# A fused decoder layer on one core: passages into and out of the attention stage, and the cross-attention scores on the two halves of the array

## The reference

```python
def reference(x, ctx_1024, ...):
    # self-attention; every row of 1024 scores gets its own maximum (softmax)
    qkv = layernorm(x) @ W_qkv + b_qkv
    energy = einsum('bqhe,bkhe->bqhk', q, k)
    attn = softmax(energy, axis=-1) / sqrt(E)
    x = x + einsum('bihv,bvhd->bihd', attn, v).reshape(B, N, E) @ W_out + b_out
    # cross-attention on 64 context tokens
    q = layernorm(x) @ Wq.T + bq ; k, v = ctx @ Wk.T + bk, ctx @ Wv.T + bv
    scores = einsum('bhqd,bhkd->bhqk', q, k) / sqrt(D_K)
    x = x + (softmax(scores, -1) @ v) @ Wo.T + bo
    # feed-forward, weights rounded to -1, 0, 1 by their mean absolute value
    h = layernorm(gelu(layernorm(x) @ absmean(W_fc).T), ln_w, ln_b)
    return x + h @ absmean(W_proj).T
```

## Time and profile before

| | us |
|---|---|
| three runs | 1186.39, 1189.93, 1192.23 (median 1189.93) |
| the profiled execution | 1189.87 |
| its span, first to last instruction | 1187.9 |
| projections, until the first unit of the attention stage | to about 129 |
| attention | about 129 to 818 |
| last stage | about 818 to 1188 |
| mean granted clock of PE | 0.991 of 2.4 GHz |

### The profile page before, as it was taken

One profiled execution on the slowest core, in us unless ns is written; L12 is line 12 of the kernel. 1 busy time (PEld: TensorE's weight loads), 2 busy tenths in 40 slices (PEclk: granted clock), 3 DMA queues, 4 the chain that ended last, 5 costly groups with the idle time before them and its releaser, 6 DMA issues.

```text
span 1187.9 us, 19073 instructions
## 1 busy us (share of the span) xinstructions
PE 1150.5 (97%) x6532; PEld 593.4 (50%) x6532; DVE 1044.4 (88%) x1974; ACT 861.9 (73%) x1898; POOL 295.6 (25%) x403
## 2 busy tenths in 40 slices
PE   8999999999999999999999999989899999999997
PEld 6544333333333333333333333344467778778777
DVE  5688799999999999999999999975799899899776
ACT  4312588888888888888888888847778778777853
POOL 2124010110110111011011000023565455455431
PEclk9999899999999999999999999989999999999999
DMA  5877113561330331333144000042111121100001
GB/s 175 261 216 233 70 26 45 132 124 21 64 59 7 64 60 29 42 60 51 20 64 66 8 10 7 11 119 61 54 37 38 54 72 34 38 19 18 2 18 36
DMA packets 45920, 74.99 MB, mean 63 GB/s; under 512 B 10112, under 2 KB 23808, under 8 KB 45824
## 3 DMA queue, kind: packets, MB, share of 16 engines
q0 software_dynamic: 9648, 27.27, 13.3%
q1 hardware_dynamic: 36176, 46.50, 12.9%
HBM read 47.53 MB, written 25.69 MB: 62 GB/s over the span
## 4 chain that ended last, share of the span: by engine, by line
PE 84%; DVE 5%; ACT 4%; issue 2%; DMA 2%; POOL 1%; SPq 1%; DVEq 0%; POOLq 0%; ACTq 0%
PE ps L1410 21%; PE ps L1423 21%; PE ps L1257 16%; PE ps L1296 10%; PE ps L1599 4%; PE ps L1519 4%; PE ps L1584 2%; PE ps L1528 2%; ACT ot L715 2%; ACT prob L652 1%; PE ps L1538 1%; DVE xhat L1150 1%; DVE maxes L883 1%; PE ps L1455 1%; ACT pe_ L727 1%
## 5 line engine op out<-in xcount | busy, mean ns | idle before, releaser
L890 DVE TENSOR_REDUCE maxes<-ps 128x1 f32<-128x512 f32 x968 | 607.9, 685 | 34.9 <-PE ps L1296 18.1
L652 ACT ACTIVATE prob<-ps 128x512 f32<-128x512 f32 x1024 | 531.9, 603 | 127.4 <-PE ps L1410 125.8
L1410 PE MATMUL ps<-Qs,Ks 50*128 50x512 f32 x1024 | 377.0, 453 | 5.5 <-DVE parts L915 1.6
L1410 PEld LDWEIGHTS ps<-Qs,Ks 50*128 50x128 f32 x1024 | 168.4, 186 | 315.3 <-ACT prob L652 300.5
L1296 PE MATMUL ps<-Ks,Qs 48*128 48x512 f32 x1024 | 319.3, 431 | 2.7 <-DVE maxes L883 2.6
L1423 PE MATMUL ps<-prob,V_all 128*32 128x512 f32 x2048 | 274.6, 608 | 0.0
L1296 PEld LDWEIGHTS ps<-Ks,Qs 48*128 48x128 f32 x1024 | 166.7, 186 | 46.2 <-DVE maxes L883 15.9
L352 POOL DMA_DIRECT2D Qs<-qk_scratch x90 | 44.4, 500 | 469.1 <-PE ps L1423 468.9
L727 ACT ACTIVATE pe_<-ps,nmx 128x64 f32<-128x64 f32 x512 | 109.7, 367 | 6.3 <-DVE nmx L1069 6.3
L566 POOL TENSOR_TENSOR pe_<-pe_,rsum 128x512 f32<-128x512 f32 x64 | 66.7, 1052 | 61.2 <-DVE rsum L1086 61.2
L1599 PE MATMUL ps<-t_p,fT 128*128 128x256 f32 x512 | 76.7, 293 | 0.0
(11 more groups left out here) (120 smaller groups left out, 1247.1 us busy)
## 6 DMA issues: line engine op xcount, KB each, us to landing
qk_scratch<-parts SPq DMA_DIRECT2D x32, 512.0 KB, 5.1
Qs<-qk_scratch POOLq DMA_DIRECT2D x90, 128.0 KB, 5.2
Ks<-qk_scratch POOLq DMA_DIRECT2D x90, 128.0 KB, 7.5
o_scratch<-ot SPq DMA_DIRECT2D x128, 32.0 KB
on_raw<-o_scratch SPq DMA_DIRECT2D x8, 512.0 KB
r_raw<-r_scratch SPq DMA_DIRECT2D x16, 256.0 KB
x_in<-in_x SPq DMA_DIRECT2D x8, 512.0 KB, 4.0
out<-xo SPq DMA_DIRECT2D x8, 512.0 KB, 2.8
```

The source lines that it names most:

```text
L652: act.activation(prob[:, U % 2, j // 2, j % 2, :], ps[:, ST_BANK[n], :], ACT.Exp).then_inc(exp_done, 1)
L890: dve.tensor_reduce(maxes[:, qc, j * BLK + blk, half:half + 1], ps[:, MAX_BANK["tile", t], :], AX.X, ALU.max).then_inc(max_reduced, 1)
L1410: pe.matmul(ps[:, ST_BANK[n], :], stack(Ks[g], j, ROWS, slice(kb * P, (kb + 1) * P)), stack(Qs[g], j, ROWS, slice(qc * CH, (qc + 1) * CH)) ...
```

## The change: what it does

1. `WARM_UP` goes from 28 to 22.
2. Entry into the attention stage: PE waits for all but the last of the projections' parts before `scores(0, 3)`; the waits for the early maxima and for the last part move into the first unit, behind `scores(1, 1)` and `scores(1, 2)`.
3. The reciprocals of the batches 0 to 2 are taken one by one inside the maxima (after tiles 952, 976 and 1000), and SP writes them ahead of the last `m_rows`.
4. `x_scores` makes two tiles at a time: the keys of heads 0 to 3 of a block lie on partitions 0 to 63 and those of heads 4 to 7 on 64 to 127, and each matmul goes over 64 partitions and 256 columns. `kbd` is half as wide. A tile now holds two row blocks x 4 heads.
5. `x1_apply` (but for chunk 0) and `x2_apply` move from DVE to ACT; POOL makes the negated mean times the factor (`nmr`) for them, two more instructions each.
6. New orders in the last stage on all engines, and a new `RING_PHASE`. On POOL, `normalise` goes from before the last of `probabilities` to between the second and third `rstd_f`; `x2_plus_b` and `x1_plus_b` go to the phase's start. `t2` and `t3` are cut in two.

```diff
-WARM_UP = 28
+WARM_UP = 22
-RING_PHASE = (("s", 2, 0), ("q2", 1, 0), ("s", 3, 0), ("s", 4, 0), ("s", 5, 0), ("s", 6, 0), ("out", 0, 1), ("out", 1, 1),
+RING_PHASE = (("q2", 1, 0), ("s", 2, 0), ("s", 3, 0), ("s", 4, 0), ("s", 5, 0), ("out", 0, 1), ("out", 1, 1), ("pt", 0, 0),
...
+RECIP_TILES = [TILES - 24 * (B - 1 - b) for b in range(B - 1)]
...
# SP, last batch
+                    if last and g == NG - 1:
+                        sp.wait_ge(recip_done, B - 1)
+                        for i in range(B - 1):
+                            r_write(i)
                     m_rows(2 * G + 1, g, 1)
                     if last and g == NG - 1:
-                        sp.wait_ge(recip_done, 1)
-                        for i in range(B - 1):
-                            r_write(i)
                         sp.wait_ge(r_written, 16 * (B - 1))
                         load_o(0, 0)
...
# POOL, rstd_2 (rstd_3 in the same way)
                 pool.tensor_tensor(veps[:, 0], mv[:, 0, :, 1], eps[:], ALU.add).then_inc(veps2_done, 1)
+                pool.tensor_tensor(nmr[:, 0], mv[:, 0, :, 0], minus[:], ALU.mult).then_inc(veps2_done, 1)
...
+                pool.tensor_tensor(nmr[:, 0], nmr[:, 0], rstd[:, 0], ALU.mult).then_inc(nmr2_ready, 1)
...
# ACT (x2_apply in the same way)
+            def x1_apply(c):
+                if not 0 < c < NCH:
+                    return
+                act.wait_ge(nmr2_ready, c + 1)
+                act.wait_ge(t2_done, 2 * c)
+                for blk in range(BLK):
+                    i = act.activation(xn_1[:, blk, :], x1[:, blk, :], ACT.Identity, scale=rstd[:, 0, blk:blk + 1],
+                                       bias=nmr[:, 0, blk:blk + 1])
+                i.then_inc(xn2_ready, 1)
...
# DVE
+            def reciprocals(b):
+                dve.wait_ge(s_loaded, 16 * max(b + 1, B - 1))
+                dve.reciprocal(s_c[:, b, :], s_c[:, b, :]).then_inc(recip_done, 1)
+
             for t in range(EARLY_TILES, TILES):
                 reduce_tile(t)
+                if t in RECIP_TILES:
+                    reciprocals(RECIP_TILES.index(t))
...
-            reciprocals(0, 0, B - 1)
...
+            dve.tensor_tensor(head_mask[:, 0:4], head_mask[:, 0:4], head_mask[:, 4:8], ALU.add).then_inc(prep_done, 1)
...
-                for h in range(8):
+                for h in range(4):
...
# PE
-            pe.wait_ge(parts_ready, 4 * NCH)
-            pe.wait_ge(max_reduced, EARLY_TILES)
+            pe.wait_ge(parts_ready, 4 * NCH - 1)
             scores(0, 3)
...
                 scores(U + 1, 1)
+                if U == 0:
+                    pe.wait_ge(max_reduced, EARLY_TILES)
                 max_tile(t + 2)
                 scores(U + 1, 2)
+                if U == 0:
+                    pe.wait_ge(parts_ready, 4 * NCH)
...
-            def x_scores(c, i):
+            def x_scores(c, t):
                 if not 0 <= c < NCH:
                     return
-                m, blk = divmod(i, BLK)
+                m, pair = divmod(t, 2)
                 pe.wait_ge(q2_copied, 2 * c + m + 1)
-                r = x_bank("s", c, i)
-                pe.matmul(ps[:, r, :], q2T[:, m, blk * P:(blk + 1) * P], kbd[:, c // QC, m * 8 * CTX:(m + 1) * 8 * CTX],
-                          start=True, stop=True).then_inc(s_done, 1)
+                r = [x_bank("s", c, 2 * t + h) for h in range(2)]
+                for k in range(2):
+                    blk = 2 * pair + k
+                    for h in range(2):
+                        rows = slice(h * STRIP, (h + 1) * STRIP)
+                        i = pe.matmul(ps[:, r[h], k * 4 * CTX:(k + 1) * 4 * CTX], q2T[rows, m, blk * P:(blk + 1) * P],
+                                      kbd[rows, c // QC, m * 4 * CTX:(m + 1) * 4 * CTX], start=True, stop=True)
+                        if k == 1:
+                            i.then_inc(s_done, 1)
```

More of the change, by code:

```diff
@@ L747, in o2_copy, with x2_apply @@
                 act.activation(o2T[:, m, :], ps[:, BANK["val", c, m], :], ACT.Copy).then_inc(o2_copied, 1)
+            def x1_apply(c):
[7 more added lines that the diff above has]
+                i.then_inc(xn2_ready, 1)
+            def x2_apply(c):
+                if not 0 <= c < NCH:
+                    return
+                act.wait_ge(nmr3_ready, c + 1)
+                if c:
+                    act.wait_ge(t3_done, 2 * c)
+                for blk in range(BLK):
+                    i = act.activation(xn_2[:, blk, :], x2[:, blk, :], ACT.Identity, scale=rstd[:, 1, blk:blk + 1],
+                                       bias=nmr[:, 1, blk:blk + 1])
+                i.then_inc(xn3_ready, 1)
             def x3_high(c, k):
@@ L1467, in t2 @@
                 pe.wait_ge(xn2_ready, c + 1)
-                for k in range(KT):
-                    transposes(x_bank("t2", c, k), k, xn_1).then_inc(t2_done, 1)
+                transposes(x_bank("t2", c, k), k, xn_1).then_inc(t2_done, 1)
             pe.wait_ge(v_copied, 2 * NCH)
@@ L1551, in t3 @@
                 pe.wait_ge(xn3_ready, c + 1)
-                for k in range(KT):
-                    transposes(x_bank("t3", c, k), k, xn_2).then_inc(t3_done, 1)
+                transposes(x_bank("t3", c, k), k, xn_2).then_inc(t3_done, 1)
             def fc(c, blk):
```

243 lines of the change are left out of this document (125 added, 118 removed), and 6 rows, old and new, of the table RING_PHASE.

## The result

The changed kernel takes 1180.87 us (median of 5 runs, 1179.83 to 1184.37) against 1189.76 for the kernel before in the same comparison: ratio 0.993, 95% interval 0.9913 to 0.9946. It is faster by 9 us, where 24.7 were forecast. The profiled execution has a span of 1180.8 us (before 1187.9).

A forecast was written before the change was run, and what follows sets the result against it. The prediction took DVE to bound attention and PE phases 2 to 6 of the last stage; its terms summed to -24.7 us from the profiled 1189.87, so 1165 us, range 1156 to 1174, or 1156 to 1182 with rivals.

The forecast's parts named there:

- the exit: From attention to the last stage: PE's wait for POOL and the slow clock behind it go, -6.2 us (bounds -3 and -8).
- phase 1: Last stage, second phase: PE's work falls to 30.6 us, 32 to 32.5 with remaining waits, -4.0 us (bounds -1, -5).
- phases 2 to 6: Last stage: PE stays the bound, but blocked f_apply leaves a phase at 42.0 us, -1.75 each, -8.7 for five.
- the end: End of the kernel: x2_apply waits for two more POOL instructions, +0.3 us.
- phase 0: Last stage, first phase: scores 2.4 us less, x1_apply ahead of the last exponentials, -2.5 us (bounds 0, -4).
- the reciprocals: In attention on DVE: taken as three of 128x128 inside the maxima and paid in full, +2.5 us (bounds +1.5, +2.7).
- the entry: Into attention: less DVE idle time before and behind its first maxima, -3.0 us (bounds -0.8 and -3.9).
- The second rival: Way out of attention: gain hidden by a later read or x1_apply(0) under POOL, -2 not -6.2 us, 1172; chance 0.10.
- Scores: Last stage on PE: the array's halves overlap, so scores take 4.0 to 4.2 us, saving 2.7 us a phase.
- the first rival: Last stage's score matmuls: halves don't overlap for two passes, scores cost 0.5 us more a phase, 1183 us; chance 0.10.
- The warm-up: Kernel start: fewer warm-up matmuls let the first transposes start earlier, carried through the projections, -1.1 us (bounds 0, -1.3).
- The rival on the slower side: Last stage: POOL blocks both f_apply of a pair, PE waits 3 us each phase, clock falls, 1199 us; chance 0.04.

## Why the prediction was wrong

The direction was right and 1180.87 lies in the range of 1156 to 1182, but the gain is little over a third of the forecast's. Of the 17.4 us that are missing in the table, 7.3 are the exit, 3.9 phase 1, 3.0 phases 2 to 6, 2.0 the end, 1.5 phase 0, 1.2 the start and 1.0 phase 7; the reciprocals gave 2.1 back and the entry 0.3.

*The exit* is the step that failed: "Late next is ACT, whose exponentials limit the last units, and DVE's `x1_apply(0)`, which ends 6 us sooner as well because `kbd` has 8 instructions and not 16." The first half came true, a projection 6.5 us earlier and without a wait. But x1_apply(0) ended only 4.9 us sooner (810.97 and 806.04), 2.9 of which had been gained before the last maximum, because an earlier `normalise` meets DVE's preparation and costs it 4.1 us, and the apply stayed at 5.45 us under POOL's second pair. So the wait of 3.57 us was in effect not removed but moved on by 13 us, and the low clock went with it. Holding POOL back shows it: 7.1 us. The second rival named this ("`x1_apply(0)` under POOL is last") and had a chance of 0.10; it was also too mild, 4.2 us lost where 7.3 were. The number that spoke for it stood in the earlier trace rows, an apply beside POOL at 4.14 us; the prediction named it for this rival and left it out of the exit's sum. The trace before had the better one, the 5.51 us of x1_apply(0) itself.

*Phase 1* failed next: "In phase 1 DVE is the chain". It was before, but the change put 4 us of applies on ACT, and in the trace after the chain runs through ACT from 853.7 to 871.8 us, with both applies in it. The saving of 2.2 us on PE turned into waits. What the runs show is partial: less ACT work gives 0.6 us, unblocking f_apply 1.0; what holds the rest is open: PE waits 1.7 us for exponentials ahead of the output projection, which the kernel before didn't, and the one other order tried was worse.

*Phases 2 to 6*: the mechanism was right and the walk nearly so. From the phase's first f_transpose gelu(0) ended at 28.3 us (forecast 28), f_apply(1) at 35.6 (35.0), f_apply(3) at 42.7 (41.9), and the phase is 42.73 (42.0). The term that was mis-sized is what PE waits: 0.6 us for `xhat` was in the sum, the 0.87 us for q2T, whose copy stands behind the same gelu(3), were not. That PE saves 2.2 us and not 2.7 made no difference while it waited. Both blocked f_apply are as foreseen; that the first one counts for 1.54 of 1.77 us was not.

*Phase 0*: ACT's apply stands on the chain, and three of its four instructions are worth 1.5 us, as much as the forecast misses; on DVE it was no better. *Phase 7*: PE's busy time fell by 2.7 us (36.84 to 34.15), but its wait for fT grew from 0.6 to 2.41; no run takes this up.

*Scores*: right. Groups of 1.06 and 2.01 us, 2.6 us a phase saved against 2.7; the first rival (no overlap) falls.

*Reciprocals*: "Whatever is put on DVE there is paid in full" is wrong. Idle time of 34.9 us in the earlier trace rows was read as too little to matter; 26 reciprocals, 24.5 us, cost a fifth of their time. That fits PE as the bound of attention, busy for 602.5 of 605 us, with DVE catching up; no run gave PE less or more work there.

*The entry* was right, in size too (-3.35), with some luck: in four of fifteen traces it is -2.0 to -2.1, and no run takes its new waits back alone. *The end* has a price of 1.5 us in the median and not 0.3: the estimate counted POOL's two instructions and not that ACT's apply takes 2.08 us where DVE's took 1.38, nor that ft_high stands behind it. *The warm-up* can't be told from the spread of a read. The rival on the slower side (waits of 3 us at each phase and a low clock) did not come: the waits were 1.47 us and the clock stayed at 1.00. Its sum was wrong too: outside the six phases the forecast's terms come to -14.0 (or -12.0 with phase 7 outside), not -9, so it would have been 1194 to 1196 and not 1199.
